# Second gelu of a pair of token tiles moved into the next block of a fused attention and feed-forward kernel, first product spread over its block

## What is computed

```python
h = layernorm(x)
q, k, v = h @ Wq.T, h @ Wk.T, h @ Wv.T        # 32 query heads, 16 key heads of 16; rope on q and k
p = softmax(q @ k.T * 16**-0.5 + causal)      # per head
attn = (p[even] - lambda_full * p[odd]) @ v   # 16 pairs of heads
x = x + (rms_norm(attn) * subln_weight * (1 - lambda_init)) @ Wo.T
w1q, w2q = ternary(w1), ternary(w2)           # -1, 0, 1 by a threshold on the mean of |w|
x = x + gelu(layernorm(x) @ w1q.T + b1) @ w2q.T + b2      # hidden size 2048
```

## Time and profile before

| | |
|---|---|
| median of the runs | 4360.22 us |
| profiled execution | 4360.82 us |
| its span, first to last instruction | 4359.0 us |
| mean granted TensorE clock | 0.913 of 2.4 GHz |
| busy, share of the span | PE 82%, DVE 78%, ACT 66%, PE weight load 49%, POOL 33% |
| gelu, L613 | 64 of 1910 ns |
| first product, L903 | 4096 matmuls |
| second product, L916 | 2048 matmuls |

### The profile page before, as it was taken

The page is one execution under the profiler, slowest core; times in us unless marked ns, Lnnn a source line. Parts: engine busy times, 40 slices in busy tenths (PEclk is TensorE's granted clock), DMA queues, the critical chain, the costliest instruction groups (busy, mean ns, idle before and its releaser), DMA issues.

```text
span 4359.0 us, 81492 instructions
## 1 busy us (share of the span) xinstructions
PE 3567.8 (82%) x23454; PEld 2128.7 (49%) x23454; DVE 3379.6 (78%) x6194; ACT 2885.3 (66%) x6786; POOL 1443.7 (33%) x1564
## 2 busy tenths in 40 slices
PE   2688888888888888888888888888988888888886
PEld 1355554455445454554545544455544555454553
DVE  6778977888678886788767887778977788678881
ACT  1577766777567775677756766667766777567782
POOL 1233233332332333322343323333133332333323
PEclk7898999999999998999899989999999999999998
DMA  3100011100001001100011000101011000111000
GB/s 128 41 19 28 19 32 33 33 14 28 30 27 33 22 25 33 32 19 28 20 32 33 30 22 23 34 23 32 19 33 32 28 19 19 33 33 32 14 28 12
DMA packets 146817, 128.38 MB, mean 29 GB/s; under 512 B 66608, under 2 KB 117680, under 8 KB 145840
## 3 DMA queue, kind: packets, MB, share of 16 engines
q1 hardware_dynamic: 146352, 122.79, 8.8%
HBM read 67.61 MB, written 55.12 MB: 28 GB/s over the span
## 4 chain that ended last, share of the span: by engine, by line
PE 45%; DVE 20%; issue 18%; ACT 11%; POOL 3%; ACTq 1%; DMA 1%; DVEq 1%; SPq 0%; POOLq 0%
PE M L831 10%; DVE NM L676 7%; PE F L916 7%; PE M L881 7%; PE F L903 6%; PE SP_ L846 6%; PE DP L858 4%; DVE NM L684 3%; ACT HP L607 3%; ACT E L552 2%; PE M L825 2%; ACT DT L564 1%; DVE CC L696 1%; PE SP_ L847 1%; ACT HP L613 1%
## 5 line engine op out<-in xcount | busy, mean ns | idle before, releaser
L552 ACT ACTIVATE E<-SP_,NM 128x256 f32<-128x256 f32 (+7 forms) x2048 | 1522.6, 744 | 965.0 <-DVE NM L684 480.4
L676 DVE TENSOR_REDUCE NM<-SP_ 128x1 f32<-128x896 f32 (+3 forms) x1024 | 1031.7, 1018 | 236.3 <-PE SP_ L847 228.5
L846 PE MATMUL SP_<-KST,QST 96*128 96x512 f16 (+3 forms) x3072 | 860.0, 353 | 355.7 <-ACT E L552 308.4
L699 DVE SCALAR_TENSOR_TENSOR E<-E,CC 128x512 f32<-128x512 f32 (+7 forms) x1024 | 929.9, 908 | 36.2
L858 PE MATMUL DP<-ident,E 128*128 128x128 f32 x3328 | 601.9, 298 | 150.3 <-ACT DT L564 80.7
L564 ACT ACTIVATE DT<-DP 128x512 f32<-128x512 f32 (+3 forms) x1024 | 524.7, 512 | 219.2 <-PE DP L858 200.7
L684 DVE TENSOR_REDUCE NM<-SP_ 128x2 f32<-128x1024 f32 (+3 forms) x512 | 420.1, 820 | 304.5 <-PE SP_ L847 299.3
L846 PEld LDWEIGHTS SP_<-KST,QST 96*128 96x128 f16 x3072 | 285.1, 103 | 694.7 <-ACT E L552 452.3
L903 PE MATMUL F<-X2H,W1Q 128*128 128x256 f16 x2048 | 496.0, 281 | 94.1 <-ACT HP L607 76.2
L858 PEld LDWEIGHTS DP<-ident,E 128*128 128x128 f32 x3328 | 402.0, 152 | 331.8 <-ACT DT L564 148.6
L831 PE MATMUL M<-WQKV,WT 128*128 128x512 f32 x1040 | 544.6, 617 | 6.3 <-DVE T L659 4.3
(11 more groups left out here) (94 smaller groups left out, 4741.2 us busy)
## 6 DMA issues: line engine op xcount, KB each, us to landing
scratch<-SPL SPq DMA_DIRECT2D x65, 576.0 KB, 2.8
QST<-scratch SPq DMA_DIRECT2D x390, 64.0 KB, 2.4
X<-in_x SPq DMA_DIRECT2D x66, 256.0 KB, 2.8
out<-SQ SPq DMA_DIRECT2D x64, 256.0 KB, 2.0
KST<-scratch SPq DMA_DIRECT2D x390, 32.0 KB, 1.9
DT<-in_w2T SPq DMA_DIRECT2D x1, 4096.0 KB, 25.8
KST<-in_w1T SPq DMA_DIRECT2D x2, 1024.0 KB, 11.4
WQKV<-in_wqT SPq DMA_DIRECT2D x1, 1024.0 KB, 6.7
```

Of the source, the lines that this page charges most:

```text
L552: act.activation(dst, score_out(i, 2 * n + k, w), ACT.Exp, bias=NM[:, (2 * u + k) % 8:(2 * u + k) % 8 + 1], scale=1.0, accum_out=SUM[:, i ...
L676: nc.vector.tensor_reduce(NM[:, m:m + 1], score_out(i, 2 * n + k, P * (i + 1)), AX.X, ALU.max, negate=True).then_inc(max_ready, 1)
L699: nc.vector.scalar_tensor_tensor(out=E1[:, u % 4, 0:w], in0=E2[:, u % 2, 0:w], scalar=CC[:, u % 4:u % 4 + 1], in1=E1[:, u % 4, 0:w], op0=A ...
L846: pe.matmul(SP_[:, k[a // 512], 0:n], q, KST[0:ROWS, a // P:(a + n) // P, kk, :], start=True, stop=not last)
```

## The change

The second gelu of a pair (hidden tiles 8 to 15) and its four splits move from half steps 25 and 26 to 29 of the odd block to half steps 0 and 1 to 4 of the even block behind it. The first gelu goes from 13 to 14, its splits to 15 to 18. The pieces of the first product start every four half steps from the fourth on. The second product of the pair's first tile starts at half step 4 rather than 3, waits at its start for the first four splits alone, and for the others ahead of f = 8 (half step 11).

```diff
-W1_AT = (1, 4, 7, 10, 13, 16, 19, 22)
-GELU = (13, 25)
-SPLIT_AT = (14, 16, 17, 18, 26, 27, 28, 29)
-W2_AT, W2_N = (3, 18), 13
+W1_AT = (1, 4, 7, 11, 15, 19, 23, 27)
+GELU_ODD, GELU_EVEN = 14, 0
+SPLIT_ODD, SPLIT_EVEN = (15, 16, 17, 18), (1, 2, 3, 4)
+W2_AT, W2_N = (4, 18), 13
...
-                    if T.w1 and hs in SPLIT_AT:
-                        hidden_split(T.pair, SPLIT_AT.index(hs))
+                    if T.w1 and hs in SPLIT_ODD:
+                        hidden_split(T.pair, SPLIT_ODD.index(hs))
+                    if T.w2 and hs in SPLIT_EVEN:
+                        hidden_split(T.pair, 4 + SPLIT_EVEN.index(hs))
...
+            def gelu(q, j):
+                after(act, hp_ready, 8 * q + 4 * j + 4)
+                act.activation(HP[:, :, :], HP[:, :, :], ACT.Gelu).then_inc(gelu_done, 1)
...
-                    if T.w1 and hs in GELU:
-                        j = GELU.index(hs)
-                        after(act, hp_ready, 8 * T.pair + 4 * j + 4)
-                        act.activation(HP[:, :, :], HP[:, :, :], ACT.Gelu).then_inc(gelu_done, 1)
+                    if T.w1 and hs == GELU_ODD:
+                        gelu(T.pair, 0)
+                    if T.w2 and hs == GELU_EVEN:
+                        gelu(T.pair, 1)
...
                 if fs[0] == 0:
-                    hold(pe, h_ready, 8 * q + 8)
+                    hold(pe, h_ready, 8 * q + 4)
                     hold(pe, hp_ready, 8 * q + 8)
                     hold(pe, o_sum, 2 * q + j)
                 for f in fs:
+                    if f == GELU_F and j == 0:
+                        hold(pe, h_ready, 8 * q + 8)
```

## The result

The changed kernel takes **4299.54 us** (median of four runs, 4298.30 to 4300.88) against 4360.5 beside it, a ratio of 0.9862 [0.9848, 0.9877]: 61 us faster, below the forecast of 4352 and below the range, which ended at 4312. It lies next to rival 2 (4302). The profiled execution has a span of 4296.5 us, where it had 4359.0. All the work is still there. First the page: its span, busy times, and the chain that ended last.

A forecast was written before the change was run, and what follows sets the result against it. No single engine was taken as the bound: four hand work to each other in order. From 4360.2 us, odd blocks 101 less, even blocks 93 more and the tail zero gave 4352, range 4312 to 4402.

The forecast's parts named there:

- rival 2: Odd blocks give more: rstd ahead of splits, clock 1.00 at ends, no waits for F; 151 less, 4302 us; chance 0.18.
- Even blocks: Second gelu at half step 0 of 30 even blocks: 81 + 15 - 9 + 6, together 93 us more.
- The first step: Head of even blocks: exponential 2's wait takes up 1.75 of the 4.47 us stall; 2.7 a block, 81 us more.
- The later second product: Even blocks, start at half step 4: 0.4 less in 23 blocks, 9 us; its later end 0.2 a block more, 6 us.
- rival 1: Head of even blocks pays more: last pair's copy later, PV at half clock; 4392 us, with both in full 4413; chance 0.25.
- the clock: Head of even blocks: TensorE idles longer ahead of PV, slowing its clock; 0.5 a block, 15 us more, between 0 and 3.2.
- Ends of odd blocks: Odd blocks from half step 25, without the second gelu and its splits: 7.45 plus 3.4, 10.85 us less a sequence.
- the comparison with the neighbours: Odd ends set against the mean of even ends around them: 0.85, -0.4, 3.25 and 3.75 us, together 7.45 a sequence.
- the piece at 27: Odd ends: 1.74 us of first product against 3.4 of second; half the difference counted, 0.85 a block, 3.4 a sequence less.
- Middle of odd blocks: Half steps 13 to 24: one piece less, waits for F included; 0.5 us a block less, between 0 and 1.74.
- the first gelu at 14: Odd blocks, first gelu moved from 13 over the half step with two projections: nothing, between -1 and +1 a block.
- Rival 3: GpSimd's splits at the head of even blocks reach past half step 7, delaying the square; 36 more, 4388 us; chance 0.08.

The follow-up runs named there:

- the kernel with the copy: The changed kernel with its second gelu, at half step 0 of the even block, made a plain copy without table loads; 4245.70 us.
- The move alone: The changed kernel with the old times of the pieces and of the first gelu, only the second gelu and its splits moved; 4326.80 us.
- the pieces alone: The changed kernel with its pieces kept, but the first gelu back at half step 13 and its splits from 14; 4322.86 us.
- the one with 44.0: The changed kernel with the last three pieces of the first product three half steps apart, at 18, 21 and 24; 4362.93 us.

## Why the prediction was wrong, step by step

**Even blocks: right in sum, by errors that cancelled.** Forecast 93 us in 30 blocks, 12.4 us a sequence with four of them; measured 11.8. The first step holds: exponential 2 without a wait, and after it the blocks are 3.1, 2.5, 2.7 and 2.8 us behind, where 4.47 - 1.75 = 2.7 stood; the 2.4 to 3.0 a block of the kernel with the copy confirm it. Three terms were mis-sized. The later second product gives 27 us and not 3, since at 3 it stands ahead of PV in a head in which PV is what everything waits for. With it at 3 the even blocks pay 14.7 us a sequence, 1.9 more than my 12.8 without this term. PV begins 3.8, 3.0, 3.4 and 3.7 us later there (tiles 0, 2, 4, 6), not 2.7, 3.1 a sequence more: that is the late copy of rival 1, whose 1.2 a block was too much (its own addends give 3.7 for that copy and not 3.9). And the clock, for which I took 2 us a sequence, costs 0.35 in PV in the changed kernel, on the mean of sequences 1 to 6: the first 32 matmuls take 1.15 us more at tile 0 and 0.1 more at tile 4, tile 2 is unchanged, and tile 6 takes 0.9 less. That all PVs would run at half clock, the 48 us of rival 1, did not come.

**Ends of odd blocks: nearly the right size, by luck.** Forecast 10.85 us a sequence from half step 25 on, measured 9.5. But the comparison with the neighbours said that a gelu at the end costs 0.85, -0.4, 3.25 and 3.75 us at tiles 1, 3, 5 and 7, 7.45 together; with twice 0.85 a block for an end without any piece that would be 14.25. The move alone gives 3.5, 2.7, 5.2 and 5.5, 16.9 of the 17.9 of four stalls (the four splits leave with the gelu). In the changed kernel 7.4 of that go again, where I counted 3.4 for the piece at 27: 3.0 is the copy of the seventh piece, now behind the boundary, and 3.2 is the wait for the stack of keys at tile 1 (none in the move alone, 1.5 us a block with the gelu at 13). Counted from exponential 24 on, tiles 3, 5 and 7 lose 0.7, 0.4 and 0.1 by it. Two estimates that were too small, of a gain and of a counter-item, gave nearly the right difference.

**Middle of odd blocks: the step that failed.** I took 0.5 us a block, 2.0 a sequence, with 1.74 a block as the most, put the waits for F in it "since the exponentials go on in most of it", and put the first gelu at 14 at nothing. Measured 9.1 a sequence to the start of exponential 25, and 6.1 without the copy that only crossed this boundary: 4.0 and 1.9 at tiles 1 and 3, -0.5 and +0.7 at 5 and 7. The move alone has none of it (it loses 0.5), and keeps 74.6 us of waits. Of the 6.1, the pieces alone give 3.6, as a gain of 4.0 and 3.3 at tiles 1 and 3 and a loss of 1.6 and 2.0 at 5 and 7. In the blocks of tiles 1 and 3 the wait for F falls by 2.3 us each, and they end 2.8 and 2.6 us earlier; at 5 and 7 it falls too, by 1.0 and 0.6, and they end 2.0 and 2.1 later. So the waits were not covered by the exponentials at tiles 1 and 3, where they had been longest (3.5 and 3.1); that each microsecond of wait became one of time is argued and not shown, and by the total of these waits the kernels don't even stand in order. What the pieces cost at 5 and 7 stays open. The rest, 3.1, is the first gelu at 14, for which I allowed -1 to +1 a block: by exponential 25 it is a cost of 0.3 and 1.4 at tiles 1 and 3 and a gain of 2.3 and 2.4 at 5 and 7, and in all 23 us. That bound was too tight as well. Why 2.3 of its 3.2 us a sequence lie in even blocks isn't known.

**The sums.** Against the forecast of 8 us less, the span fell by 62.5. Odd blocks in seven sequences account for 41 of the 54 between them (18.65 for 12.85), the first sequence for 8, even blocks for 4, the tail for 2. By edits the 5.8 a sequence in the odd blocks part otherwise: the move gives 16.4 where my terms without a piece at the end make 14.25, the pieces give 1.3 where they cost 1.4 in my sum (2.0 less 3.4), and the gelu at 14 gives 0.9 where I had nothing. Rival 2 had the sum of 4302 and two of its three grounds: fewer waits for F and a clock near 1.00 at the ends. Its third, the rstd held up behind the splits, brought nothing by itself: what splits two half steps later gave the odd ends they took from the heads. I gave it 0.18 for the reason that the end of tile 3 is no longer than its neighbours', and that was the comparison that fell.

**Rival 3** had its sign at one tile and not its price. The margin of the square is down to 1.7 us at tile 0 and to none at tile 2, but the block of tile 2 is 2.5 us longer, no more than the stall less the wait. With the gelu at 3 the square waits for nothing in any even block of the loop, and that kernel is the fastest.

## What to carry to other kernels

A stall of an in-order engine costs at least what no wait directly behind it takes up, so put it ahead of the engine's longest wait: the same 4.47 us cost 1.1 us in the head of a block at half step 3, 3.0 at 0 and 4.6 at 4. What such a wait is worth is read from the timeline of that engine, row by row, and not from blocks beside it that hold other work. Where a product goes through a single accumulator tile, don't price its waits by their total: the kernel with 74.6 us of them is 36 us faster than the one with 44.0. Look at what stands behind each one on TensorE, and try the places: moving a single piece by one step cost 28.5 and 23.7 us here, where moving the gelu brought 34.

## What the runs showed of the hardware

A table load for the gelu and the one back took 1.28 us each, and the rows around them follow within 0.02 us; 62 of them taken out gave 75 us. The mean granted clock doesn't tell one kernel's time from another's: with the gelu at 4 it is 0.925, as after the change (0.926), and the time is 92 us more. Within one kernel it does go with the time: the runs with the first gelu at 13 took 4325.77 us at 0.914 and 4311.83 at 0.922. So a part of a difference of 10 or 20 us here may be clock, and no run holds the clock fixed.
